# Layer 0's scan: the decayed state made on VectorE inside the step, sigmoids by tanh, a second product buffer, and one group's inputs moved later

## The reference, cut to what matters

```
# layer 0: a gated delta rule over the tokens; the 4 x 512 tokens are read as 512 positions of a batch of 4
a  = sigmoid(x @ Wa.T + ba);  b = sigmoid(x @ Wb.T + bb)          # one of each per token and head (16 heads of 8)
def step(S, (q, k, v, a, b)):                                     # S: 8 x 8 per batch item and head
    Sk = einsum('bhde,bhe->bhd', S, k)
    S  = a*S - a*b*outer(Sk, k) + b*outer(v, k)
    return S, einsum('bhd,bhde->bhe', q, S)                       # the output o of this token
x = x + ga * (o @ Wo.T + bo)

# both mixtures of experts: top 2 of 8 (layer 0) or 16 (layer 1) experts, softmax over the two kept scores
w, i = top_k(softmax(h @ gate_w.T), 2);  w = w / sum(w)
x = x + gb * sum_k w_k * expert_{i_k}(h)
```

## Time and profile before

| | us |
|---|---|
| median of three runs | 1365.88 |
| lowest, highest | 1353.64, 1368.22 |
| the profiled execution's own time | 1352.62 |
| its span, from the first to the last instruction | 1350.9 |
| its mean granted TensorE clock | 0.850 |
| busy in it: TensorE, VectorE, ScalarE, GpSimd | 989.0, 846.5, 623.9, 442.6 |

### The profile page before, as it was taken

The page is one execution under the profiler, slowest core; times in us unless marked ns, Lnnn a source line. Parts: engine busy times, 40 slices in busy tenths (PEclk is TensorE's granted clock), DMA queues, the critical chain, the costliest instruction groups (busy, mean ns, idle before and its releaser), DMA issues.

```text
span 1350.9 us, 18007 instructions
## 1 busy us (share of the span) xinstructions
PE 989.0 (73%) x5924; PEld 600.3 (44%) x5924; DVE 846.5 (63%) x2008; ACT 623.9 (46%) x1485; POOL 442.6 (33%) x636
## 2 busy tenths in 40 slices
PE   5563074985886896888788888878788878775682
PEld 3231032443453454333334555544556545544582
DVE  1386978858988332675666566766566666624452
ACT  3435253464444253154444456643556534663272
POOL 0201352634633323022442331363241444422413
PEclk9776595996997998787888899987999988998796
DMA  7000000000000001000000323212134003331372
GB/s 221 1 0 1 0 0 1 1 1 35 1 1 1 1 0 36 1 1 1 1 1 1 114 71 105 75 36 92 33 111 122 29 18 120 106 107 46 125 218 80
DMA packets 53885, 64.67 MB, mean 48 GB/s; under 512 B 6544, under 2 KB 38304, under 8 KB 53792
## 3 DMA queue, kind: packets, MB, share of 16 engines
q1 hardware_dynamic: 51744, 59.33, 14.6%
q0 software_dynamic: 2048, 4.20, 1.0%
HBM read 52.83 MB, written 10.68 MB: 47 GB/s over the span
## 4 chain that ended last, share of the span: by engine, by line
PE 46%; DVE 19%; issue 13%; ACT 11%; POOL 8%; DMA 2%; SPq 0%; DVEq 0%; POOLq 0%; ACTq 0%
PE banks L701 8%; PE banks L844 4%; PE banks L758 4%; DVE MX L1323 3%; PE banks L554 3%; PE banks L776 3%; POOL oms L1796 3%; PE banks L748 2%; PE banks L818 2%; PE banks L711 2%; PE banks L714 2%; PE banks L606 2%; POOL QX L1695 2%; PE banks L723 2%; ACT PT L1620 1%
## 5 line engine op out<-in xcount | busy, mean ns | idle before, releaser
L1323 DVE TENSOR_REDUCE MX<-banks 128x4 f32<-128x512 f32 (+2 forms) x192 | 199.3, 1044 | 87.2 <-PE banks L818 86.5
L1774 POOL TENSOR_SCALAR_AFFINE_SELECT PT<-PT 128x256 f32<-128x256 f32 x256 | 107.0, 432 | 419.4 <-ACT PT L1620 419.1
L1620 ACT ACTIVATE PT<-banks 128x768 f32<-128x768 f32 (+1 forms) x192 | 167.9, 876 | 92.6 <-PE banks L776 91.5
L701 PE MATMUL banks<-xgT,wg 128*128 128x128 f32 x736 | 106.3, 290 | 36.1 <-ACT ysb L1581 29.5
L701 PEld LDWEIGHTS banks<-xgT,wg 128*128 128x128 f32 x736 | 92.5, 198 | 57.7 <-issue 53.0
L844 PE MATMUL banks<-PT,VA 128*17 128x512 f32 (+3 forms) x1024 | 98.4, 482 | 13.6 <-DVE on L1346 13.6
L783 PE MATMUL banks<-KS,QS 32*128 32x512 f32 (+3 forms) x512 | 96.7, 421 | 14.7 <-DVE MX L1323 12.3
L776 PE MATMUL banks<-QS,KS 32*128 32x128 f32 (+3 forms) x512 | 91.7, 407 | 15.0 <-ACT PT L1620 9.6
L748 PE MATMUL banks<-w,hid 128*128 128x128 f32 x512 | 76.1, 296 | 30.6 <-DVE hid L1268 28.5
L748 PEld LDWEIGHTS banks<-w,hid 128*128 128x128 f32 x512 | 69.6, 206 | 63.3 <-DVE hid L1268 43.9
L1272 DVE SCALAR_TENSOR_TENSOR sil<-sil,yh 128x256 f32<-128x256 f32 x124 | 53.4, 431 | 62.7 <-ACT sil L1567 62.4
(11 more groups left out here) (256 smaller groups left out, 2120.8 us busy)
## 6 DMA issues: line engine op xcount, KB each, us to landing
wg<-in_ffn_dram SPq DMA_DIRECT2D x92, 386.0 KB, 3.4
xg<-xs SPq DMA_DIRECT2D x20, 256.0 KB, 3.1
yb<-ysb SPq DMA_DIRECT2D x20, 256.0 KB, 3.9
w<-in_ffn_w_dram SPq DMA_DIRECT2D x12, 256.0 KB, 5.0
xs<-zt SPq DMA_DIRECT2D x1, 1472.0 KB, 11.1
x<-in_L_attn_x_dram SPq DMA_DIRECT2D x4, 256.0 KB, 5.0
out_dram<-x SPq DMA_DIRECT2D x16, 64.0 KB, 1.5
wmod<-in_L_wmod_dram SPq DMA_DIRECT2D x2, 384.0 KB, 4.1
```

Source lines behind the costliest of these rows:

```text
L701: mm = e.matmul(ps[:, at:at + cols], w, h, start=True, stop=True)
L1323: v_mx.at(e.tensor_reduce(MX[n % 2][:, u:u + nm, qb % 2, 2 * pair:2 * pair + 2, 24].rearrange("p s i -> p i s"), p4, AX.X, ALU.max, negate ...
L1620: a_p.at(e.activation(PT[q % 3][:, 2 * pair:2 * pair + 2, :], where["score", q, pair][:, :, 0:n], ACT.Exp, scale=ISQ8))
L1774: ins = e.affine_select(out=pt, in_=pt, compare_op=ALU.is_ge, fill=0.0, base=0, pattern=[[0, 2], [1, 128]], channel_multiplier=-1)
```

## The change

1. **Decayed state.** ScalarE's operation L1518 and its signal `a_ts` are gone. VectorE makes the fifth column of `T2` itself with a `tensor_scalar` of 32 elements (a per-partition factor), placed between the first product and the sum that depends on it; its signal is `v_ts`.
2. **Sigmoids by tanh.** `decay` is tanh(x/2), `share` one operation (times 0.5 plus 0.5). In the routing the difference of the two best scores (`gd`) goes through tanh in part 2, and the two weights `gk` are 0.5 -/+ 0.5 tanh. The subtraction over all scores, the masked product, its sum, the reciprocal and, in layer 1, the picking out of the weights are gone; a product of the two one-hot masks with `gk` and a sum of the two stand in their place.
3. **Two product buffers.** The second half of group 3's products goes to the memory of `Z[0]`, which no convolution reads any more by then (`p_cv` 10), so it doesn't wait for TensorE's sum of the first half.
4. **Read-out.** `o_gq` waits for `v_gm` and no longer for the last state; for group 3 it and the other steps stand earlier in the table.
5. **Order.** `input_table(3)` moves from `SCAN[0] + 36` to `SCAN[0] + 68`; VectorE's offsets of `ab`, `up`, `route` and `o_x` change.

```diff
 LATE0 = dict(
     PE=dict(norm=1.5),
-    DVE=dict(mod=1.0, gate=1.0, ab=1.0, up=5.0, route=1.0, o_x=1.0),
+    DVE=dict(mod=1.0, gate=1.0, ab=6.0, up=6.0, route=2.0, o_x=2.0),
...
-        gq, state, pw, dk, ol, sums, out, step = 0, (1, 6), 1, 6.5, 7, (6, 12, 15), 17, 1.3
+        gq, state, pw, dk, ol, sums, out, step = -10, (0, 5), 0, 5.5, 6, (5.5, 10.5, 13.5), 15, 1.3
...
-    table += input_table(2, SCAN[0] + 2) + input_table(3, SCAN[0] + 36)
+    table += input_table(2, SCAN[0] + 2) + input_table(3, SCAN[0] + 68)
...
+        QXs = [QX[:, :, :, :], Z[0][:, :, :].rearrange("p b t -> p (b t)")[:, 0:2048].rearrange(
+            "p (t r e) -> p t r e", r=4, e=4)]
...
             def share(g):
                 abf = ab[:, g, :, :]
                 v.wait_ge(a_dx, g + 1)
-                n = v_own.at(e.tensor_scalar(abf, abf, 1.0, None, ALU.add))
-                v.wait_ge(v_own, n)
-                v_dec.at(e.reciprocal(abf, abf))
+                v_dec.at(e.tensor_scalar(abf, abf, 0.5, 0.5, ALU.mult, ALU.add))
...
                 n = v_own.at(e.tensor_tensor(T1[k1][:, :, :, 0:8], S_[:, c, :, :].unsqueeze(2).broadcast_to([128, 4, 4, 8]),
                                              XU[:, c, :, 0:8].unsqueeze(1).broadcast_to([128, 4, 4, 8]), ALU.mult))
+                v_ts.at(e.tensor_scalar(t2[:, :, :, 4], S_[:, c, :, :], GMb[g % 2][:, c, 3:4], None, ALU.mult))
                 v.wait_ge(v_own, n)
                 v.wait_ge(a_val, j + 1)
                 v_w.at(e.tensor_reduce(W_[:, c, :, :], T1[k1][:, :, :, :], AX.X, ALU.add))
...
-                v.wait_ge(a_ts, j + 1)
+                v.wait_ge(v_ts, j + 1)
...
-                a_rx.at(e.activation(gq2[:, :, 0:E], gq2[:, :, 0:E], ACT.Exp))
+                a_rx.at(e.activation(gd[:, :], gd[:, :], ACT.Tanh, scale=0.5))
...
-                a_dx.at(e.activation(ab[:, g, :, :], ab[:, g, :, :], ACT.Exp, scale=-1.0))
+                a_dx.at(e.activation(ab[:, g, :, :], ab[:, g, :, :], ACT.Tanh, scale=0.5))
...
-                a.wait_ge(v_gm, g + 1)
-                a.wait_ge(g_zero, 1)
-                a.wait_ge(v_s, j)
-                a_ts.at(e.activation(T2[c % 2][:, :, :, 4], Sb[g % 2][:, c, :, :], ACT.Copy, scale=GMb[g % 2][:, c, 3:4]))
                 if c + 3 < 32:
                     values(j + 3)
...
-                g_.wait_ge(v_s, 32 * g + 32)
+                g_.wait_ge(v_gm, g + 1)
...
-                g_.wait_ge(p_o, 2 * g + eh)
+                g_.wait_ge(v_s, 32 * g + 32)
+                if g == 3 and eh:
+                    g_.wait_ge(p_cv, 10)
+                else:
+                    g_.wait_ge(p_o, 2 * g + eh)
```

More of the change, by code:

```diff
@@ L274, in build @@
         gq = sb("gq", [128, 4, 16])
-        gq2 = sb("gq2", [128, 4, 16])
+        gd = sb("gd", [128, 4])
+        gk = [sb(f"gk{i}", [128, 2, 4]) for i in range(2)]
         go = sb("go", [128, 2, 4, 16])
@@ L365, in build @@
         gX = sb("gX", [128, 2, 4, 16])
-        gk = [sb(f"gk{i}", [128, 2, 4]) for i in range(2)]
         gc = sb("gc", [128, 16, 4])
@@ L605, in o_sum @@
                     for k in range(4):
-                        mm = e.matmul(ps[64 * part:64 * part + 64, :], sumh[:, :], QX[:, :, k, :], start=(k == 0), stop=False,
+                        mm = e.matmul(ps[64 * part:64 * part + 64, :], sumh[:, :], QXs[g == 3 and part][:, :, k, :], start=(k == 0), stop=False,
                                       skip_group_check=True)
```

55 lines of the change are left out of this document (21 added, 34 removed).

## The result

The changed kernel takes 1355.51 us (median of 20 runs, 1348.45 to 1364.42) against 1365.88 (20 runs, 1353.22 to 1372.18) before: a ratio of 0.9933, 95% interval 0.9911 to 0.9955. It is 0.7% faster where 3% was forecast. The profiled execution has a span of 1346.6 us at a mean clock of 0.848, against 1350.9 and 0.850. Within it layer 0's last expert matmul ends at 518.7 where it ended at 524.5, so layer 0 gained 5.8 us; layer 1 took 827.9 against 826.4.

A forecast was written before the change was run, and what follows sets the result against it. The scan's chain through VectorE was taken as the bound, then TensorE's expert list. Gains of 55 us less costs of 23 made net 32, 1352.6 to 1320.6 (1333 from the median); forecast 1325 us, between the two, range 1302 to 1348.

The forecast's parts named there:

- I take all 38.1 as gone.: In the scans: VectorE's waits for ScalarE's decayed state, 38.1 us, would all go.
- I take 0.08 a step, 10 us: In each scan step: VectorE's new operation would lengthen the step by 0.08 us, 10 us over 128 steps.
- I take 8.: In the scans: GpSimd's bursts would hold VectorE's new operation for 8 us, between nothing and 15.
- I put 5 us, between 0 and 15.: In the scans: a faster VectorE would newly wait 5 us for what TensorE, ScalarE and GpSimd deliver.
- Gates' matmuls, 6.7.: In the scans: VectorE's waits for the gates' matmuls, 6.7 us, would all go with group 3's inputs later.
- Reciprocals 3.0 and 1.3 ahead of the scan.: Sigmoids by tanh: three reciprocals fewer in the scans save 3.0 us; 1.3 us more is saved ahead of them.
- 48 in place of 54.3, a gain of 6: From the scans' end to the last experts' start: 44 us of TensorE work at full clock plus 4 of waits.
- one level of two: Basis: runs would lie on the profiled execution's level or 12 to 15 us higher; the forecast lay between.
- GpSimd's lock and late ScalarE eat half: Rival in the scans: net gain 11 us, 1342 in the profiled run's terms; chance 0.24 together with the kept hand-over.

The follow-up runs named there:

- e2: The changed kernel with the decayed state back on ScalarE; ratio to the kernel before 0.9994, scans 346.7 us.
- e5: The changed kernel with the new operation in a form that also writes a sum nobody reads; ratio to the kernel before 0.9884, scans 334.8 us.
- e12: The changed kernel with group 3's inputs and the offset of `ab` where they were before; ratio to the kernel before 1.0000.
- e11: The changed kernel with the gates by exp and reciprocal again, the routing keeping tanh; ratio to the kernel before 0.9999.
- e4: The changed kernel with the old table row for group 3's read-out and the single product buffer; ratio to the kernel before 0.9943.
- e15: The changed kernel with the accumulating form, `up` at 5 and VectorE's group 3 read-out one unit later; ratio to the kernel before 0.9775.
- e6: The changed kernel with VectorE's offset of `up` back at 5; ratio to the kernel before 0.9863.

## Why the prediction was wrong

The direction held, the size didn't: 32 us of net gain were forecast, and the medians differ by 10.4, the spans by 4.3. By its own steps:

- *"I take all 38.1 as gone."* Right: the wait is zero in the changed kernel. e2 shows that the table loads hadn't caused it.
- *The operation's pitch, "I take 0.08 a step, 10 us".* Too high: an undisturbed step grew by 0.04 us, the lower end, 5 us over 128 steps. The sum behind the operation starts 0.36 after the first product (149.81 to 150.17), just under the 0.37 to 0.46 that was given.
- *Held by GpSimd, "I take 8."* **This step failed**: the stretching grew by 15.9 us, the upper end of 15. The row behind the lower value said that two operations per step already lose only 30 us, as if holds were rare. The rule cited there, by which the plain form is held like the products, was right, and the row of `xn` at 1281 ns had shown it. e5 shows the cause. Pitch and hold together are 21 us against the 18 taken; so far that is an error of 3.
- *New waits, "I put 5 us, between 0 and 15."* **This step failed by more.** The waits other than the hand-over and the gates' went from 3.4 (48.2 - 38.1 - 6.7) to 17.6 (19.4 - 1.8), so 14.2 us. They are single waits: `hid` for ScalarE's `sil` 5.7 in three and for TensorE's matmuls 4.8 in four, `p` for ScalarE's `AB` 2.0, and `gsg` 3.8, of which 2.6 stood there before. The share of 72.5 of 87 us that TensorE was busy said that it wouldn't be the bound, and it isn't. But average slack says nothing of the moment at which VectorE asks.
- *Gates' matmuls, 6.7.* Nearly right: 1.8 us of such waiting is left, a gain of 4.9, and e12 loses 5.8 us of scan without it.
- *Reciprocals 3.0 and 1.3 ahead of the scan.* Right: 2.9 less on VectorE, the first step 1.5 earlier (72.8 against 74.3), and e11 finds 1.6 of this again. What else changed in routing and elsewhere, put at nothing, added about 1 us in the scans, and GpSimd held `xn` for 3.1 us more, which no term had foreseen.
- *The tail (from the scans' end to the last experts), "48 in place of 54.3, a gain of 6".* **This step failed with its sign**: 56.5 us. I had written that TensorE's wait for `hid1` "rather grows by 2 to 3 us" and then let a full clock (44 us of work) and 4 us of waits outweigh it. The clock in that window is 0.91, not 1, and TensorE stood idle for 9.11 us at once in it. The wait grew by 5.5 us, twice what was said, since the twelve operations ahead of `hid1` took 1.07 us each on average beside GpSimd's ten unbroken microseconds. The six of before took 1.09 each (426.87 to 433.42), so it is their number that grew, not the price of one. The new read-out isn't what made the tail longer: without it (e4) the tail is 2.5 us longer still. e15 puts `hid1` ahead of half of the twelve and gains 5.2 us. The offset of `up`, for which the sum had no term, brought three of the six added operations and 1.4 us (e6).
- *Offsets.* The sum had no term for `up` from 5 to 6. e6 puts it at 6.6 us of scan and 8.7 of layer 0 in this kernel. It is no separate loss: it is part of the stretching, the waits and the tail above.

In the scans: gains 38.1 + 4.9 + 2.9 = 45.9, costs 14.2 in new waits and, with the reciprocals set apart, 24.9 in occupied time (20.7 in the steps' five operations, 3.1 in `xn`, about 1 elsewhere), which leaves 6.8; the scans shrank by 6.3 (the occupied times reach a little over the ends of the scans). With 1.5 ahead of them and 2.0 lost behind them (100.2 against 98.2 from the scans' end to L0) that is the 5.8 of layer 0. Against the 32 forecast, 26 are missing: 9 in new waits, 8 in the tail, 3 in the new operation, 3 in `xn`, 2 in the gates' matmuls and 1 in routing.

The rest is the basis. I took the profiled execution's 1352.6 as one level of two. The changed kernel's profiled execution, 1348.45, is its fastest of 20, so a single execution says little about the median: the medians are 13.3 us above it before and 7.1 after. About 6 of the 10.4 us between the medians aren't in the two traces. Of the rivals, "GpSimd's lock and late ScalarE eat half" had the mechanism, hold and new waits at 15 and 12. Its 1342 in the profiled run's terms comes near the 1348.45 by some luck: its pitch of 17 us was 12 too high, which covered most of the 8 that it missed in the tail and the 6 in `xn`, the gates' matmuls and routing.

## What to carry to other kernels

Before work is moved onto an engine to save a hand-over, price it as if it stood beside the other engine's bursts, and look for a form that isn't held: here an unused accumulator on the same operation took 10.9 us off layer 0, and the ratio went from 0.9933 to 0.9884. Count what the faster engine will ask for earlier: of 38 us of removed waiting, 14 came back as short waits, nine of them, for engines with slack on average. And where TensorE's list is the bound, don't put twelve operations ahead of the one that it waits for; one table unit there was worth 5 us.
